# The first sequence of an attention stage in an order of its own, on one Trainium2 core

## The chip, the cores and the metric

The kernel runs on one core of a Trainium2 chip: TensorE (PE, matrix products into PSUM), VectorE (DVE), ScalarE (ACT), GpSimd (POOL), and SyncE (SP), which here only issues transfers. The metric is the device time of one execution in microseconds.

## The reference

Input x has 8 sequences of 512 tokens of 128 features. Four blocks follow, each with a layer norm before and after it and a residual. The second layer's attention is what the change is about:

```python
x = x + _layernorm(_L0_attn_ref(_layernorm(x), ...))    # a GRU with 256 hidden units over 512 steps
x = x + _layernorm(_L0_ffn_ref(_layernorm(x), ...))     # top-1 of 8 experts with low-rank parts
x = x + _layernorm(_L1_attn_ref(_layernorm(x), ...))    # below
x = x + _layernorm(_L1_ffn_ref(_layernorm(x), ...))     # SwiGLU
...
q, k, v, p, y = jnp.split(proj, ...)                    # 256 each, y: one gate for each of 16 heads
k = (1 - smear) * k + smear * k_prev
pos = jnp.cumsum(jax.nn.sigmoid(y).transpose(0, 2, 1), axis=-1)
mask = causal - (pos[..., :, None] - pos[..., None, :])
attn = softmax(q / s @ (k / s) / 4 + mask)
out = (silu(p) * (attn @ v)) @ W_out.T
```

## The kernel before

The program has three blocks, with all engines meeting between them. The first turns the GRU's weights. The second runs the recurrence, 16 steps a group, 32 groups; beside it runs the expert layer, which leaves finished rows in the tile XM, a group at a time (signal x_done), 16 steps by 8 sequences on the partitions. SyncE writes each group to the DRAM tensor x_steps and after eight groups reads a quarter of X back (L656, L661), with tokens on the partitions.

The third block is attention, sequence by sequence (b, with p = b % 2 its buffer). Its order is written out by hand in `sequences`: each engine calls the same steps, and each step has its instructions under a slot number i from 0 to 43. For a sequence there are:

- project_qk: statistics, XN (normalized rows), XT (turned), four products (two halves of q, two of k), the smearing of k on DVE (KK), and the gates, whose running sums become the columns KA and, turned, KAT.
- split (GpSimd): a float32 half becomes three bfloat16 parts, by two casts and two subtractions (PQ, PK).
- The stacks QS and KS: for each head 96 rows of parts in six orders, and rows for positions and maxima. SyncE's `project` writes parts to DRAM (q_parts, k_parts, k_extra) and reads them back turned, six loads of 256 KB for each stack. All count on one semaphore for each buffer, stack_in[p], which TensorE's `stacks` waits for as a whole before the first head.
- project_v: values and gates of the output; its bias bv3 is split in seven DVE operations (value_bias).
- maxima: for a group of four heads, 11 score products (L1730), each reduced by DVE (L2143); max_parts and rows_of_maxima bring the maxima into QS (ScalarE).
- The body of a sequence: exponentials and products with values, with the maxima two groups ahead; in its slots stand project_v of the next sequence and project_qk of the one after.

`start` does sequence 0's and 1's projections and the first two groups' maxima before the first body.

## Time and profile before

| | us |
|---|---|
| median of 3 runs | 1723.03 (1718.81 to 1726.69) |
| the profiled execution | 1728.01 |
| its span | 1726.3 |
| granted TensorE clock, mean | 0.655 |

The span is the time from first to last instruction of the one profiled execution; a clock of 1.00 is 2.4 GHz, 0.50 is 1.2 GHz. The recurrence takes the first 1053 us of the span, attention and the last block the rest.

### The profile page before, as it was taken

The page shows a single profiled execution, that of the slowest core. Times are in us where ns is not written, and L with a number is a line of the kernel's source. Part 1 is how long each engine was busy: PE and PEld are TensorE (multiplying, and loading weights), DVE is VectorE, ACT ScalarE, POOL GpSimd, SP SyncE. Part 2 cuts the span into 40 slices and gives each one's busy share as a digit, 9 for nine tenths or more (in the row PEclk, how much of TensorE's full clock was granted, in tenths as well). Part 3 has the DMA queues.
Part 4 walks back from the last instruction along what each step waited for, and adds up shares of the span by engine and source line. Part 5 has one row for each costly group of instructions (what it writes and reads, how often), then busy time and mean ns, then how long its engine had stood idle before and what let it go on. Part 6 is the DMA issues. An engine that isn't in the chain of part 4 may idle for free.

```text
span 1726.3 us, 65445 instructions
## 1 busy us (share of the span) xinstructions
PE 1403.0 (81%) x27370; PEld 1028.4 (60%) x27370; DVE 1182.0 (68%) x5759; ACT 688.4 (40%) x2427; POOL 411.8 (24%) x700
## 2 busy tenths in 40 slices
PE   5788888888888888888888774489999999988896
PEld 4677777777777777777777652245545555544443
DVE  5667777777777777777777764466577677566475
ACT  3333232222222222222222221147566666665765
POOL 2011111111111111111111124521441442411254
PEclk6555555555555555555555555679899999998898
DMA  5200000000000000000000001882563663660001
GB/s 116 25 4 5 6 5 5 6 17 7 5 5 6 5 17 6 5 7 5 5 18 5 7 6 34 103 129 33 86 87 50 94 87 48 96 87 9 1 13 37
DMA packets 68363, 55.77 MB, mean 32 GB/s; under 512 B 11086, under 2 KB 67302, under 8 KB 68070
## 3 DMA queue, kind: packets, MB, share of 16 engines
q1 hardware_dynamic: 65894, 51.41, 19.7%
q8 instruction: 215, 3.52, 0.9%
q10 hardware_dynamic: 2176, 0.20, 0.1%
q14 instruction: 78, 0.64, 0.1%
HBM read 33.93 MB, written 17.56 MB: 30 GB/s over the span
## 4 chain that ended last, share of the span: by engine, by line
PE 55%; DVE 24%; ACT 10%; issue 7%; DMA 2%; POOL 1%; SPq 0%; POOLq 0%; DVEq 0%; ACTq 0%
PE PS L716 33%; ACT tz L922 6%; DVE GB L1026 6%; DVE zg L1019 5%; PE PS L1776 5%; DVE zn L1022 4%; PE PS L1730 4%; PE PS L1746 3%; DVE MX L2143 3%; PE PS L1678 2%; ACT PT L1957 1%; PE PS L1733 1%; PE PS L1717 1%; PE PS L1749 1%; PE PS L1832 1%
## 5 line engine op out<-in xcount | busy, mean ns | idle before, releaser
L716 PE MATMUL PS<-GB,W 128*128 128x8 f16 x18432 | 575.6, 168 | 178.9 <-DVE GB L1026 174.2
L716 PEld LDWEIGHTS PS<-GB,W 128*128 128x128 f16 x18432 | 532.4, 104 | 287.6 <-DVE GB L1026 282.3
L2143 DVE TENSOR_REDUCE MX<-PS 128x1 f32<-128x512 f32 (+3 forms) x352 | 221.7, 635 | 162.8 <-PE PS L1733 160.7
L920 ACT ACTIVATE tr<-PS 128x16 f32<-128x16 f32 x512 | 93.7, 183 | 490.9 <-PE PS L716 490.9
L1957 ACT ACTIVATE PT<-PS 128x512 f32<-128x512 f32 (+1 forms) x352 | 193.1, 562 | 172.6 <-PE PS L1749 169.0
L1730 PE MATMUL PS<-KS,QS 99*128 99x256 bf16 (+3 forms) x512 | 138.6, 323 | 51.1 <-DVE MX L2143 23.7
L1012 DVE SCALAR_TENSOR_TENSOR u_<-tr,PS 128x16 f32<-128x16 f32 x512 | 87.7, 171 | 125.8 <-PE PS L716 114.2
L922 ACT ACTIVATE tz<-PS 128x16 f32<-128x16 f32 x512 | 93.7, 183 | 193.7 <-PE PS L716 193.7
L670 POOL TENSOR_TENSOR rt<-mv,eps 128x1 f32<-128x1 f32 x96 | 18.2, 190 | 553.9 <-DVE mv L1037 553.9
L1019 DVE SCALAR_TENSOR_TENSOR zg<-tz,HR 128x16 f32<-128x16 f32 x512 | 89.8, 175 | 80.6 <-ACT tz L922 80.5
L1746 PE MATMUL PS<-QS,KS 102*128 102x256 bf16 (+3 forms) x512 | 134.4, 314 | 2.8 <-ACT PT L1957 2.4
L729 PE MATMUL PS<-Y,V 128*128 128x32 f16 x2322 | 130.9, 188 | 0.0
L1730 PEld LDWEIGHTS PS<-KS,QS 99*128 99x128 bf16 x512 | 46.6, 104 | 124.7 <-DVE MX L2143 51.3
L724 PE MATMUL PS<-ones,brow 128*128 128x32 bf16 x1032 | 110.3, 188 | 2.1 <-PEq L194 2.1
L924 ACT ACTIVATE n_<-v_ 128x16 f32<-128x16 f32 x512 | 110.3, 215 | 0.4 <-DVE v_ L1016 0.2
L1776 PE MATMUL PS<-PT,VV 128*32 128x512 f32 (+3 forms) x1024 | 103.3, 477 | 1.2 <-ACT PT L1957 1.2
L1029 DVE TENSOR_TENSOR GB<-HR,GB 128x16 f16<-128x16 f32 x512 | 89.7, 175 | 17.5
L1026 DVE SCALAR_TENSOR_TENSOR GB<-zg,zn 128x16 f16<-128x16 f32 x512 | 89.5, 175 | 17.6
L1016 DVE TENSOR_TENSOR v_<-u_,PS 128x16 f32<-128x16 f32 x512 | 87.4, 171 | 17.5
L729 PEld LDWEIGHTS PS<-Y,V 128*128 128x128 f16 x2322 | 98.7, 104 | 0.0
L1733 PE MATMUL PS<-maskU,identb 128*128 128x128 bf16 x512 | 91.6, 231 | 0.0
L1022 DVE SCALAR_TENSOR_TENSOR zn<-tz,n_ 128x16 f32<-128x16 f32 x512 | 89.8, 175 | 0.6 <-ACT n_ L924 0.2
(362 smaller groups left out, 2519.2 us busy)
## 6 DMA issues: line engine op xcount, KB each, us to landing
QS<-q_parts SPq DMA_DIRECT2D x48, 256.0 KB
KS<-k_parts SPq DMA_DIRECT2D x48, 256.0 KB
q_parts<-PQ SPq DMA_DIRECT2D x16, 384.0 KB, 13.3
k_parts<-PK SPq DMA_DIRECT2D x16, 384.0 KB, 13.9
x_steps<-XM SPq DMA_DIRECT2D x32, 64.0 KB, 1.5
out_dram<-X SPq DMA_DIRECT2D x8, 256.0 KB, 2.3
X<-x_steps SPq DMA_DIRECT2D x4, 448.0 KB
XM<-in_L_attn_x_dram SPq DMA_DIRECT2D x16, 80.0 KB
```

Of the source, the lines that this page charges most:

```text
L716: return pe.matmul(bank[:, p, at:at + B], W[:, kc, w:w + P], state[:, part, kc, :], start=False, stop=True, skip_group_check=True)
L724: pe.matmul(o, brow[:, (bias + mc) * P:(bias + mc + 1) * P], ones3[:, :], start=start and mc == 0, stop=False, skip_group_check=True)
L729: pe.matmul(o, V[:, w], Y[:, rows], start=False, stop=False, skip_group_check=True)
L922: act.activation(as_states(tz), now(pZ), ACT.Tanh, scale=gate_scale).then_inc(tz_ready.sem, 1)
L1019: dve.scalar_tensor_tensor(zg[:, :], tz[:, :], 1.0, before, ALU.add, ALU.mult).then_inc(zg_ready.sem, 1)
L1022: dve.scalar_tensor_tensor(zn[:, :], tz[:, :], 1.0, n_[:, :], ALU.subtract, ALU.mult).then_inc(zn_ready.sem, 1)
L1026: dve.scalar_tensor_tensor(high, by_chunk(zg[:, :]), 0.5, by_chunk(zn[:, :]), ALU.mult, ALU.subtract).then_inc(g1_ready.sem, 1)
L1730: pe.matmul(bank[:, a * w:(a + 1) * w], QS[0:KM, p, 4 * g + i, q], KS[0:KM, p, 4 * g + i, 0:w], start=(a == 0), stop=False, skip_group_che ...
L1746: pe.matmul(bank[:, a * w:(a + 1) * w], KS[0:KF, p, 4 * g + i, j * P:(j + 1) * P], QS[0:KF, p, 4 * g + i, j * P:S], start=(a == 0), stop=F ...
L1776: last = pe.matmul(p_o[32 * i:32 * i + 32, j * P:S], VV[:, p, j, 4 * g + i, :], PT[:, j % 2, i, 0:S - j * P], start=(j == 0), stop=(j == N ...
L1957: act.activation(PT[:, j % 2, heads[0]:heads[-1] + 1, 0:w], p_e[:, k % 2, 0:len(heads) * w].rearrange("p (a w) -> p a w", w=w), ACT.Exp).t ...
L2143: dve.tensor_reduce(MX[:, g % 2, heads[0]:heads[-1] + 1, NT - 1 - it], p_x[:, k % 2, 0:len(heads) * w].rearrange("p (a w) -> p a w", w=w), ...
```

## The change

1. Finished rows go from XM to X by one transfer within SBUF for each group; the DRAM tensor is gone. SyncE's program in the second block ends when all have landed.
2. Sequence 0 has steps of its own, `first_sequence` on each engine and `project_first` on SyncE. The products go q half 0, k half 0, gates, q half 1, k half 1, into banks of their own. GpSimd splits the two q halves, DVE the two k halves.
3. The stacks of sequence 0 are read by heads: 0 to 3, 4 to 7, and 8 to 15, with a semaphore for each (the second uses x_done's, so it prints as x_rows_ready); k_extra is written and read between them.
4. value_bias runs on DVE in two pieces, around XN. The constants (tri, ones, masks) are made in the first block; KA and QA are set by DVE, VV by GpSimd between its two splits.
5. In `start`, sequence 1's project_qk comes behind the maxima of group 0 and is interleaved with those of group 1.

The core of the diff (before.py to after.py):

```diff
                 for u in range(NG):
                     sp.wait_ge(x_done.sem, u + 1)
-                    sp.dma_start(xs_d[u * GS:(u + 1) * GS].rearrange("t b d -> (t b) d"), XM[:, u, :]).then_inc(x_out.sem, 16)
-                    k = u // (NG // NT)
-                    if u % (NG // NT) == NG // NT - 1:
-                        sp.wait_ge(x_out.sem, 16 * (u + 1))
-                        for first, n, back in ((0, 1, x_back0), (1, B - 1, x_back)):
-                            sp.dma_start(X[:, k * B + first:k * B + first + n, :],
-                                         xs_d[k * P:(k + 1) * P, first:first + n, :]).then_inc(back.sem, 16)
+                    k, first = u // (NG // NT), (u % (NG // NT)) * GS
+                    sp.dma_start(X[first:first + GS, k * B:(k + 1) * B, :].rearrange("p n d -> p (n d)"),
+                                 XM[:, u, :]).then_inc(x_back.sem, 16)
+                sp.wait_ge(x_back.sem, x_back.value(sp, NG - 1))
...
                 def start():
-                    for i in range(SLOTS):
-                        project_qk(0, 0, i)
+                    first_sequence()
                     for i in range(SLOTS):
                         project_v(0, 0, i, None)
-                    for i in range(SLOTS):
-                        project_qk(1, 1, i)
                     for j in range(NT):
                         for n in range(len(ITEMS[j])):
                             maxima(0, 0, 0, j, n)
                     for k in range(NI):
                         max_parts(0, 0, 0, k)
                         rows_of_maxima(0, 0, 0, k, None)
-                    for j in range(NT):
-                        for n in range(len(ITEMS[j])):
-                            maxima(0, 0, 1, j, n)
+                    items = [(j, n) for j in range(NT) for n in range(len(ITEMS[j]))]
+                    for i in range(SLOTS):
+                        project_qk(1, 1, i)
+                        if i % 4 == 3:
+                            maxima(0, 0, 1, *items[i // 4])
...
+                def project_first():
+
+                    def out(c, parts, done, dram, src):
+                        sp.wait_ge(parts.sem, parts.value(sp, 0, 4 * (c + 1)))
+                        sp.dma_start(dram[0][:, c * P:(c + 1) * P, :].rearrange("s p n -> p s n"), src[:, c, :, :]).then_inc(done.sem, 16)
+
+                    def back(dst, dram, order, heads, done):
+                        for r, part in enumerate(order):
+                            sp.dma_start(dst[r * DH:(r + 1) * DH, 0, heads, :],
+                                         dram[0][part].rearrange("(h d) n -> d h n", d=DH)[:, heads, :]).then_inc(done.sem, 16)
+                    q_order, k_order = (0, 0, 0, 1, 1, 2), (0, 1, 2, 0, 1, 0)
+                    h0, h1, h23 = slice(0, 4), slice(4, 8), slice(8, HEADS)
+                    out(0, parts_q, q_out, qd, PQ)
+                    out(0, parts_k, k_out, kd, PK)
+                    sp.wait_ge(q_out.sem, 16)
+                    back(QS, qd, q_order, h0, first_in[0])
+                    sp.wait_ge(k_out.sem, 16)
+                    back(KS, kd, k_order, h0, first_in[0])
+                    out(1, parts_q, q_out, qd, PQ)
+                    sp.wait_ge(kaT.sem, kaT.value(sp, 0))
+                    sp.dma_start(ad[0], KAT[:, :]).then_inc(a_out.sem, 16)
+                    back(QS, qd, q_order, h1, first_in[1])
+                    sp.wait_ge(a_out.sem, a_out.value(sp, 0))
+                    sp.dma_start(KS[96:KF, 0, :, :], ad[0].rearrange("(h r) n -> r h n", r=6)).then_inc(first_in[0].sem, 16)
+                    back(KS, kd, k_order, h1, first_in[1])
+                    out(1, parts_k, k_out, kd, PK)
+                    sp.wait_ge(q_out.sem, 32)
+                    back(QS, qd, q_order, h23, stack_in[0])
+                    sp.wait_ge(k_out.sem, 32)
+                    back(KS, kd, k_order, h23, stack_in[0])
...
+                def first_sequence():
+                    scales(0)
+                    split(0, 0)
+                    pool.memset(VV[:, :, :, :, DH:32], 0.0).then_inc(acon.sem, 1)
+                    pool.wait_ge(acon.sem, 9)
+                    pool.memset(VV[:, :, :, :, DH:DH + 1], 1.0).then_inc(acon.sem, 1)
+                    split(0, 1)
+                    scales(1)
...
+                def first_sequence():
+                    pe.wait_ge(xn.sem, xn.value(pe, 0))
+                    for t in range(NT):
+                        last = pe.transpose(p_b[:, t * P:(t + 1) * P], XN[:, t, :], ident[:, :])
+                    last.then_inc(xnT_ps.sem, 1)
+                    pe.wait_ge(xnT.sem, xnT.value(pe, 0))
+
+                    def product(c, bank):
+                        pe.matmul(PS[:, bank, :], winT[:, c * P:(c + 1) * P], XT[:, 0, :], start=True, stop=True).then_inc(qk_ps.sem, 1)
+                    product(0, 7)
+                    product(2, 0)
+                    for t in range(NT):
+                        last = pe.matmul(p_a[:, t * HEADS:(t + 1) * HEADS], XT[:, 0, t * P:(t + 1) * P], winT[:, 4 * DE:], start=True, stop=True)
+                    last.then_inc(y_ps.sem, 1)
+                    product(1, 1)
+                    product(3, 2)
+                    pe.wait_ge(acon.sem, 8)
+                    pe.wait_ge(sg.sem, sg.value(pe, 0))
...
                 def stacks(b, p, g):
-                    if g == 0:
-
-                        loaded = b * (STACK_DMAS * 8) + (STACK_DMAS * 16 - STACK_DMAS * 8 * p + 16)
-                        pe.wait_ge(stack_in[p].sem, loaded if isinstance(b, int) else pe.snap(loaded))
+                    if b == 0 and g < 2:
+                        pe.wait_ge(first_in[g].sem, first_in[g].value(pe, 0))
+                    if g == (2 if b == 0 else 0):
+                        loaded = STACK_DMAS * 16 * (b // 2 + 1)
+                        pe.wait_ge(stack_in[p].sem, loaded + 16 if p else loaded - 16)
...
+                def first_sequence():
+                    act.wait_ge(xnT_ps.sem, xnT_ps.value(act, 0))
+                    act.activation(XT[:, 0, :], p_b, ACT.Identity, scale=ilw[:, 0:1], bias=ilb[:, 0:1]).then_inc(xnT.sem, 1)
+
+                    def queries(c, bank):
+                        act.wait_ge(qk_ps.sem, qk_ps.value(act, 0, 1 + turn(0, c)))
+                        act.activation(QF[:, c, :], PS[:, bank, :], ACT.Identity, scale=qsc[:, 4 + c:5 + c], bias=bqs[:, c:c + 1]).then_inc(qk.sem, 1)
+
...
+                    act.wait_ge(yb.sem, yb.value(act, 0))
+                    act.activation(SG[:, :, :], YB[:, :, :], ACT.Tanh, scale=0.5).then_inc(th.sem, 1)
+                    queries(1, 1)
+                    keys(1, 2)
...
+                dve.memset(KA[:, :, :, :], 1.0).then_inc(acon2.sem, 1)
+                dve.memset(QA[:, :, :, :], 1.0).then_inc(acon2.sem, 1)
+                value_bias((0, 1, 2))
...
+                def first_sequence():
+                    dve.wait_ge(arst.sem, arst.value(dve, 0))
...
+                    value_bias((3, 4, 5, 6))
+
+                    def smear(c):
+                        dve.wait_ge(qk.sem, qk.value(dve, 0, 1 + turn(0, 2 + c)))
...
+                    def split(c):
+                        rest = PT[:, 0, 3, :]
...
+                    smear(0)
+                    dve.wait_ge(y_ps.sem, y_ps.value(dve, 0))
+                    dve.tensor_tensor(YB[:, :, :], p_a[:, 0:NT * HEADS].rearrange("p (t h) -> p t h", t=NT),
+                                      bvpy[:, 2 * DE:].unsqueeze(1).to_broadcast([P, NT, HEADS]), ALU.add).then_inc(yb.sem, 1)
+                    split(0)
+                    dve.wait_ge(th.sem, th.value(dve, 0))
+                    dve.tensor_scalar(SG[:, :, :], SG[:, :, :], 0.5, 0.5, ALU.mult, ALU.add).then_inc(sg.sem, 1)
+                    smear(1)
```

SyncE (SP), at the first sequence's stacks, before; the shapes are partitions x heads x tokens:

```order
L1489 DMA q_parts<-PQ 128x3x512 [waits parts_ready] x2
L1492 DMA k_extra<-KAT 96x512 [waits kaT_ready]
L1497 DMA QS<-q_parts 16x16x512 [waits q_parts_to_dram]
L1497 DMA QS<-q_parts 16x16x512 x5
L1500 DMA k_parts<-PK 128x3x512 [waits parts_ready] x2
L1503 DMA KS<-k_extra 6x16x512 [waits k_extra_to_dram]
L1506 DMA KS<-k_parts 16x16x512 [waits k_parts_to_dram]
L1506 DMA KS<-k_parts 16x16x512 x5
```

and after:

```order
L1525 DMA q_parts<-PQ 128x3x512 [waits q_parts_ready]
L1525 DMA k_parts<-PK 128x3x512 [waits k_parts_ready]
L1529 DMA QS<-q_parts 16x4x512 [waits q_parts_to_dram]
L1529 DMA QS<-q_parts 16x4x512 x5
L1529 DMA KS<-k_parts 16x4x512 [waits k_parts_to_dram]
L1529 DMA KS<-k_parts 16x4x512 x5
L1525 DMA q_parts<-PQ 128x3x512 [waits q_parts_ready]
L1541 DMA k_extra<-KAT 96x512 [waits kaT_ready]
L1529 DMA QS<-q_parts 16x4x512 x6
L1544 DMA KS<-k_extra 6x16x512 [waits k_extra_to_dram]
L1529 DMA KS<-k_parts 16x4x512 x6
L1525 DMA k_parts<-PK 128x3x512 [waits k_parts_ready]
```

What was one chain of whole stacks is now three pieces, the first two of four heads each.

DVE, from the first smearing of k, before (PT is a borrowed tile that holds the value bias's parts):

```order
L2099 TENSOR_SCALAR KK<-KF_,qsc 128x512 [waits qk_ready]
L2102 SCALAR_TENSOR_TENSOR KK<-KF_,qsc,KK 128x511 [waits k_scaled]
L2099 TENSOR_SCALAR KK<-KF_,qsc 128x512 [waits qk_ready]
L2102 SCALAR_TENSOR_TENSOR KK<-KF_,qsc,KK 128x511 [waits k_scaled]
L2057 CAST PT<-bvpy 128x512
L2059 TENSOR_TENSOR PT<-bvpy,PT 128x512 [waits v_bias_parts]
L2061 CAST PT<-PT 128x512 [waits v_bias_parts]
L2063 TENSOR_TENSOR PT<-PT 128x512 [waits v_bias_parts]
L2065 TENSOR_SCALAR PT<-PT,ident 128x512 [waits v_bias_parts]
L2067 SCALAR_TENSOR_TENSOR PT<-PT,ident 128x512 [waits v_bias_parts]
L2069 SCALAR_TENSOR_TENSOR bv3<-PT,ident 128x512 [waits v_bias_parts]
```

and after, from the rest of value_bias behind XN:

```order
L2145 TENSOR_TENSOR PT<-PT 128x512 [waits v_bias_parts]
L2147 TENSOR_SCALAR PT<-PT,ident 128x512 [waits v_bias_parts]
L2149 SCALAR_TENSOR_TENSOR PT<-PT,ident 128x512 [waits v_bias_parts]
L2151 SCALAR_TENSOR_TENSOR bv3<-PT,ident 128x512 [waits v_bias_parts]
L2218 TENSOR_SCALAR KK<-KF_,qsc 128x512 [waits qk_ready]
L2220 SCALAR_TENSOR_TENSOR KK<-KF_,qsc,KK 128x511 [waits k_scaled]
L2235 TENSOR_TENSOR YB<-PS,bvpy 128x64 [waits y_ps]
L2226 CAST PK<-KK 128x512 [waits k_smeared]
L2228 TENSOR_TENSOR PT<-KK,PK 128x512 [waits k_parts_ready]
L2230 CAST PK<-PT 128x512 [waits k_parts_ready]
L2232 TENSOR_TENSOR PK<-PT,PK 128x512 [waits k_parts_ready]
L2239 TENSOR_SCALAR SG<-SG 128x64 [waits gate_tanh_ready]
```

The value bias stood between the smearing and KA; it now stands ahead, and the split of a key half has come to DVE, ahead of SG.

PE, at the end of sequence 1's projections and the first score product (PS<-KS,QS), before:

```order
L1697 MATMUL PS<-identb,KA 96x128 [waits ka_ready,qk_ready]
L1697 MATMUL PS<-identb,KA 96x128 x3
L1730 MATMUL PS<-KS,QS 128x512 [waits stacks_in0]
L1733 MATMUL PS<-maskU,identb 128x128
L1730 MATMUL PS<-KS,QS 128x512
L1733 MATMUL PS<-maskU,identb 128x128
L1730 MATMUL PS<-KS,QS 128x512 [waits max_ready]
```

and after, from the turned maxima of group 0 (identb,QA) on:

```order
L1815 MATMUL PS<-identb,QA 128x128 [waits max_parts_ready]
L1815 MATMUL PS<-identb,QA 128x128 x3
L1692 MATMUL PS<-ident,XN 128x128 [waits xn_ready,silu_ready]
L1692 MATMUL PS<-ident,XN 128x128 x3
L1786 MATMUL PS<-KS,QS 128x512 [waits max_ready,x_rows_ready]
L1789 MATMUL PS<-maskU,identb 128x128
L1700 MATMUL PS<-winT,XT 128x16 [waits xnT_ready,silu_ready]
L1700 MATMUL PS<-winT,XT 128x16 x3
L1707 MATMUL PS<-XT,winT 128x512
L1786 MATMUL PS<-KS,QS 128x512 [waits max_ready]
L1789 MATMUL PS<-maskU,identb 128x128
L1707 MATMUL PS<-XT,winT 128x512 [waits yb_ready]
```

Sequence 1's projections stood ahead of the first score product; now they stand behind the 11 of group 0, with those of group 1 between their steps.

## Rows read from the trace of the kernel before

**Rows 1.** Chain that ended last in order of time (start us, us, what), stretch 1080:1330.

```profile
1087.96 0.60 ACT KAT L1936
...
1088.98 1.04 SPq L1497
...
1093.01 14.22 DMA k_parts<-PK
...
1109.60 13.21 DMA KS<-k_parts
...
1122.85 0.61 PE PS L1730
```

**Rows 2.** Timeline, 1096 to 1172: start us, us, engine line op, idle before.

```profile
1096.15 1.11 DVE L2087 TENSOR_SCALAR XN<-X,MV,RR 128x128 f32<-128x128 f32 x4
...
1114.00 0.59 ACT L1936 ACTIVATE KAT<-PS 96x512 bf16<-96x512 bf16 x1 [6.50 <-PE PS L1697]
...
1133.47 2.42 ACT L1946 ACTIVATE QS<-PS 6x512 bf16<-6x512 bf16 x4 [18.88 <-PE PS L1759]
...
1141.75 0.63 PE L1746 MATMUL PS<-QS,KS 102*128 102x512 bf16 x1
...
1171.21 0.38 PE L1730 MATMUL PS<-KS,QS 99*128 99x512 bf16 x1
```

**Rows 3.** Timeline, 1052 to 1068, all engines and SyncE's queue.

```profile
1052.93 0.32 SPq L656 DMA_DIRECT2D x_steps<-XM  x1
...
1054.47 0.80 SPq L661 DMA_DIRECT2D X<-x_steps  x2
...
1056.31 0.87 DVE L2049 BATCH_NORM_STATS2 STa<-X 128x6 f32<-128x128 f32 x4 [0.44 <-DMA X<-x_steps]
...
1059.15 2.48 DVE L2087 TENSOR_SCALAR XN<-X,MV,RR 128x128 f32<-128x128 f32 x4 [1.54 <-POOL RR L139]
...
1059.17 1.80 POOL L1534 MEMSET VV<- 128x2048 f32 x1
...
1063.73 1.89 PE L1671 MATMUL PS<-winT,XT 128*128 128x16 f32 x8 [0.93 <-ACT XT L1919]
...
1065.45 6.64 PE L1678 MATMUL PS<-XT,winT 128*128 128x512 f32 x8
...
1067.54 0.78 ACT L1925 ACTIVATE QF<-PS,bqs,qsc 128x512 f32<-128x512 f32 x1 [3.87 <-PE PS L1678]
```

**Rows 4.** One line's instructions in all: duration ns min/median/max.

```profile
L1568 POOL TENSOR_TENSOR RES<-QF,PQ x16: 1152/1157/1476, 1069.2 to 1477.4; 128x512 f32<-128x512 f32 x16
...
L1570 POOL CAST PQ<-RES x16: 609/610/720, 1070.5 to 1478.7; 128x512 bf16<-128x512 f32 x16
...
L2099 DVE TENSOR_SCALAR KK<-KF_,qsc x16: 473/475/1394, 1071.7 to 1482.1; 128x512 f32<-128x512 f32 x16
```

**Rows 5.** Stretches: length, busy us of each engine, granted clock, DMA share, GB/s.

```profile
core 0: us, PE busy (x) PEld busy (x) DVE busy (x) ACT busy (x) POOL busy (x), PEclk, DMA share, GB/s
...
1097.00:1101.00 4.00, 2.64 (x13) 2.46 (x14) 0.37 (x2) 0.78 (x1) 0.00 (x0) 0.72 1.15 115
...
1130.00:1142.00 12.00, 9.49 (x47) 4.50 (x48) 8.75 (x17) 2.35 (x4) 0.00 (x0) 0.50 1.04 154
...
1144.00:1148.00 4.00, 3.75 (x28) 2.39 (x28) 3.43 (x10) 3.10 (x7) 0.00 (x0) 1.00 1.16 116
```

**Rows 6.** Tile q_parts: time of its writes from issue to landing.

```profile
DMA to landing us min/median/max: 2.5/13.3/14.2
```

**Rows 7.** Timeline: SyncE's stack loads of sequences 1 and 2, TensorE's wait.

```profile
1124.51 2.80 SPq L1497 DMA_DIRECT2D QS<-q_parts  x6
...
1141.73 2.80 SPq L1506 DMA_DIRECT2D KS<-k_parts  x6
...
1197.09 2.85 SPq L1497 DMA_DIRECT2D QS<-q_parts  x6
...
1232.03 0.59 PE L1730 MATMUL PS<-KS,QS 99*128 99x512 bf16 x1 [1.95 <-issue]
```

180 lines of the change are left out of this document (109 added, 71 removed).

## The prediction

> **What bounds the kernel now.** I read the page first: a profiled execution of 1728.0 us, span 1726.3 (the table above). The recurrence of the first layer takes the first 1053 us, and nothing of the change costs time in it. So I read the chain of work that ended last only behind it, in order of time. There the chain leaves the engines: ScalarE copies KAT, the position rows of the keys, at 1087.96, SyncE issues the query loads at 1089.0, then come 14.2 us of the transfer k_parts and 13.2 us of the transfer into KS, and TensorE's first score product starts at 1122.85 [rows 1]. From 1089.0 to 1122.85, 33.9 us, TensorE does the value projection and sequence 1's projections, and then it stands still. The reader is to see that one thing ends that stretch: all 16 heads of both stacks must have landed before the first head is scored. The steady part (from 1141.75, exp products of sequence 0 on TensorE [rows 2]) is TensorE's own, and the change leaves it as it is; so what counts is when it starts, and whether sequence 1's stacks are there when it asks for them.
>
> **The row transfers.** Before, the last rows went to DRAM at 1052.93, had landed when the loads back were issued at 1054.47 (1.54 us), and DVE's statistics started at 1056.31 [rows 3]. After, one transfer of 64 KB within SBUF, and SyncE ends its program when it has landed. No row shows such a transfer; I take the 1.54 us of its neighbour. The other engines then start some 0.8 us earlier (the two issues of rows 3 are gone), and the statistics at about 1055.2: 1.1 us gained. Bounds: 0 (it lands 1.1 us later) and 1.4. The deletions inside the recurrence are hidden beside 2 us steps that do not wait for SyncE: nothing. The constants of GpSimd go to the first block, behind its last work there: at most a fraction of a microsecond of DVE contention, taken as nothing.
>
> **Up to the first parts.** XN starts at 1059.15 and its four pieces take 2.48, since GpSimd's clearing of VV (1.80) starts beside them [rows 3]; sequence 1's four take 1.11 [rows 2]. After, DVE does two memsets and three value-bias steps in the wait (some 2.5 us by estimate, 0.5 each, against 1.54 of waiting), so XN starts near 1059.4 and ends at 1060.5 instead of 1061.6. Transposes and XT take what they took (2.1 us), the first product no longer stands behind the gate products (they start at 1063.73, the first product at 1065.45 [rows 3]: 1.7 us), so QF is there 2.8 us earlier, at 1064.75 instead of 1067.54. GpSimd splits the first query half in two casts of 0.61 and two subtractions of 1.15 to 1.48 with gaps [rows 4]: done at 1069.9. The first key half follows in 1.7 us on TensorE (four products in 6.64 [rows 3]): KF_ at 1067.2, smeared by DVE at 1069.4. Its split on DVE is four operations of the kind of L2099, 0.475 alone and 1.39 beside GpSimd [rows 4]; VV's 1.8 us memset now lies beside them. I take 1.2 each with gaps: done at 1074.4; bounds 1071.5 and 1076.5. KA follows at 1079.1, the second key half at 1081.9, moments at 1083.2. So KAT comes 8 us earlier, at 1080.
>
> **The first stack.** A write of one half (384 KB) lands in 2.5 us when nothing is ahead of it, and the loads run at 115 GB/s [rows 5, 6]. Four heads of QS are 384 KB: 3.4 us at that rate, and as six issues 2.8 us of SyncE (six took 2.80 [rows 7]). In the order of the queue: q half written 1070.0, k half 1074.5, QS heads 0 to 3 issued 1075.0 to 1078.0, KS of them to 1080.9, second query half, k_extra at 1081.5, QS heads 4 to 7 to 1084.5; the wait for k_extra in DRAM ends near 1085.5, and KS's rows of it, behind 384 KB in the queue, land near 1090.5. TensorE comes to the scores at about the same time: KA is there at 1079, but DVE takes the value projection up only at 1083.3, and its four chunks end at 1090. First score product 1090.5 instead of 1122.85. The heads 4 to 15 (2.3 MB) are all in by 1104, ahead of their use.
>
> **What takes the time back.** Sequence 1's projections ran inside the old wait; now they stand behind the maxima of the first four heads. From the first score product to the last row of maxima on ScalarE are 13.0 us (1122.85 to 1133.47 + 2.42 [rows 1, 2]): 1103.5. There ScalarE takes XT of sequence 1; from there to KAT were 15.9 us (1098.1 to 1114.0, XN's end plus 0.8 [rows 2]), now with six maxima between the steps. Eleven took at most 13.0 - 2.4 = 10.6 us, 0.96 each; I count half of that, since the rest falls into waits (bounds: nothing and all, 0 and 5.8): KAT at 1122.3. Five more maxima, 3.7 us: the steady part starts at 1126.0 instead of 1141.75, 15.7 us earlier. Next is late: sequence 1's stacks. They are asked for 29.5 us behind the start (1141.75 to 1171.21 [rows 2]), so at 1155.5. From the issue of the query loads to their landing were 33.9 us for sequence 0 [rows 1] and 34.9 for sequence 2 (1197.09 to 1232.03, where TensorE waited 1.95 [rows 7]); sequence 1's KS was issued 17.2 us behind its first issue (1124.51, 1141.73 [rows 7]), which with 14.3 us to land makes 31.5. With the first issue at 1122.6, behind KAT: 1154.1 to 1157.5, a wait of 0 to 2. I take 1. The 15 us of slack that sequence 1 had are spent.
>
> **The sum.** 15.7 - 1 = 14.7, some 15 us: 1713.3 for a profiled execution like the one of 1728.0, which stood 5.0 above the median; so 1708 for the median of 1723.0.
>
> **The rivals.**
> 1. The forecast, 11 to 19 us gained (1704 to 1712): 0.54.
> 2. More, 19 to 26 us (about 1700). TensorE's granted clock was 0.50 (1.2 GHz) while it alternated with DVE in the maxima and 1.00 (2.4 GHz) in the steady part [rows 5]. With the projections and maxima of heads 4 to 7 interleaved it is fed more densely; at the high level their 22 us shrink by 3 or 4, and the six maxima may hide wholly (3). Against: sequence 1's stacks move by this only as far as KAT does. 0.13.
> 3. The small loads cost more. Each of the 24 loads of four heads is 64 KB. If such a load took 0.95 us of the queue instead of the 0.56 that 115 GB/s gives, the 12 ahead of the first score product would end 4.7 us later: 10 us gained, 1713. With the issues also stretched, or the wait for k_extra longer, 5 to 11 gained (about 1714). 0.17. For: the queue is a chain of four round trips here. Against: twelve issues hide the load.
> 4. Sequence 1's stacks come 4 to 9 us late, since the writes of its key halves stand behind 1.5 MB of query loads (14.2 us to land [rows 1]): 5 to 10 gained, 1715. 0.10. It is decided by KAT of sequence 1: every microsecond past 1122 in it counts once.
> 5. Slower. The interleaved projections stretch, because each hop between engines now waits behind a maximum on DVE and TensorE, and KAT of sequence 1 comes so late that its stacks land behind 1171.2, when they were asked for before. That decides from KAT at 1137 on; at 1147 the kernel ends 10 us later, 1733. Against: six maxima at 0.96 us are 5.8 us, so it would take over three times their length. 0.03.
> 6. Nothing: the wait for the first stack is only renamed (first_stacks_in lands past 1110): 1720. 0.03.
>
> Beside rival 3: the Trainium skill, "DMA: Bandwidth & Descriptors", section "Measured (HBM→SBUF, 128 partitions, SWDGE, issued from GpSimd)", gives 0.95 us for 64 KB and advises transfers of 1 MiB or more, which speaks against cutting the loads. By it the sum would be 10 instead of 15. These are SyncE's queues, and the trace has 256 KB loads at 115 GB/s, far under that page's rate for such sizes, so I leave it the smaller chance.
>
> **How the numbers follow.** Runs of this kernel spread by 0.5%, 8.6 us, which is also about what a measurement can tell from no change. Cases 1 and 2 are faster by more (0.67), and of cases 3 and 4 (0.27) somewhat under half: 0.78 faster, 0.19 the same, 0.03 slower. The range goes from 1699, which takes in most of rival 2, to 1718, which takes in rivals 3 and 4 and the spread of the runs; it leaves out cases 5 and 6 and the tail of 2, about 0.12.
>
> **What would show it.** Right: the first score product near 1090, released by KS (k_extra) or by the value projection within 3 us of each other; KAT of sequence 1 at 1120 to 1124; the first exp product at 1124 to 1128; the first maxima of sequence 1 behind a wait of 0 to 2 us; from there a constant shift. Wrong: a first score product past 1097 (rival 3), a wait over 4 us for sequence 1's stacks (rival 4), KAT past 1130 (rival 5), or DVE's split of the first key half past 1077, which would put every transfer off.

## The result, and the profile after

Measured together, the changed kernel took 1708.67 us (median of 6 runs, 1701.6 to 1716.0) and the kernel before 1724.86 (6 runs, 1717.39 to 1727.86): a ratio of 0.9923, 95% interval 0.9894 to 0.9952. That is 13.3 us won (8 to 18) by the ratio, 16.2 by the medians. The forecast was 1708.

The page of the changed kernel's profiled execution (1701.6 us) shows that its engines do the same work; the queue q1 has fewer bytes, since the row transfers no longer go through DRAM, and the clock row reads 9 in the recurrence, where the execution before read 5 (the last line is that of before):

```profile
PE 1397.2 (82%) x27355; PEld 1028.8 (61%) x27370; DVE 1180.2 (69%) x5769; ACT 688.0 (40%) x2427; POOL 404.3 (24%) x690
...
PEclk9999999999999999999999999789999999999898
...
q1 hardware_dynamic: 65126, 49.31, 18.7%
```

```profile
PEclk6555555555555555555555555679899999998898
```

The timeline at the entry of the attention block, changed kernel (start us, us, engine line op):

```profile
1051.23 0.45 POOL L712 TENSOR_TENSOR XM<-XM,N 128x128 f32<-128x128 f32 x1 [0.18 <-POOL N L709]
...
1051.70 0.55 SPq L675 DMA_DIRECT2D X<-XM  x1
...
1054.60 0.87 DVE L2127 BATCH_NORM_STATS2 STa<-X 128x6 f32<-128x128 f32 x4
...
1058.21 1.11 DVE L2211 TENSOR_SCALAR XN<-X,MV,RR 128x128 f32<-128x128 f32 x4
```

The recurrence ends with the addition to XM, at 1051.68 here and at 1052.90 before. To compare executions, every mark below is counted from there. Statistics start 2.92 us behind it instead of 3.41 [rows 3], and XN's four pieces take 1.11 us instead of 2.48.

The timeline of the same execution at the marks that the prediction named; a bracket holds the idle time ahead and what ended it:

```profile
1086.98 0.39 PE L1786 MATMUL PS<-KS,QS 99*128 99x512 bf16 x1 [2.83 <-DMA KS<-k_extra]
...
1097.33 2.42 ACT L2024 ACTIVATE QS<-PS 6x512 bf16<-6x512 bf16 x4 [12.30 <-PE PS L1815]
...
1116.35 0.59 ACT L1994 ACTIVATE KAT<-PS 96x512 bf16<-96x512 bf16 x1 [6.38 <-PE PS L1724]
...
1121.09 0.63 PE L1802 MATMUL PS<-QS,KS 102*128 102x512 bf16 x1
...
1153.79 0.38 PE L1786 MATMUL PS<-KS,QS 99*128 99x512 bf16 x1
```

The first score product came at 1122.85 [rows 1] and comes at 1086.98, where the extra key rows are the last thing it waits for (2.8 us). The first exp product came at 1141.75 and the first maxima of sequence 1 at 1171.21 [rows 2]; now 1121.09 and 1153.79. So 35.9 us are won at the first score product, 20.7 at the first exp product and 17.4 at sequence 1's maxima (1.2 of each is the recurrence's). The stretch between the last two marks, called the body below, covers the first two of sequence 0's four groups of four heads. It grew from 29.5 to 32.7 us: 2.7 us of that is TensorE standing idle (1.3 us before, 4.0 now), 0.5 us is its busy time. The chain in order of time says what it stood idle for, which had not been foreseen:

```profile
1082.84 4.09 DMA KS<-k_extra
...
1120.92 0.62 POOL PK L1590
1121.61 1.17 POOL PK L1592
1123.24 1.03 POOL RR L146
1124.30 0.60 DVE XN L2171 x2
1124.90 0.61 DVE MX L2272
1125.64 0.58 PE PS L1786
```

```profile
1125.64 0.58 PE L1786 MATMUL PS<-KS,QS 99*128 99x512 bf16 x1 [2.67 <-DVE MX L2272]
```

The last step of GpSimd's splits of sequence 1, before:

```profile
1119.85 1.15 POOL L1572 TENSOR_TENSOR PK<-RES,PK 128x512 bf16<-128x512 f32 x1
```

Before, these splits ended 20.7 us ahead of the first exp product; now they run from 1105.6 to 1122.8 and end 1.7 us behind it. Behind them on GpSimd stand the scales of sequence 2; DVE waits for these with XN, and behind XN in DVE's order stands the maximum that TensorE waits 2.67 us for.

### The profile page after: what moved, and what is told of

Same layout as the page of the kernel before. It is cut to its first block and busy times, and to the rows that moved or that the text cites. A ratio compares the mean times of both kernels' runs of the same rounds, so it can differ in the third digit from the quotient of the medians.

```text
span 1699.8 us, 65434 instructions
## 1 busy us (share of the span) xinstructions
PE 1397.2 (82%) x27355; PEld 1028.8 (61%) x27370; DVE 1180.2 (69%) x5769; ACT 688.0 (40%) x2427; POOL 404.3 (24%) x690
```

## The experiments

Each kernel is the changed one with one edit, unless said otherwise. The marks, in us from the end of the recurrence, one profiled execution each; "body" is the last mark less the one ahead of it, with TensorE's mean granted clock in it and the longest single wait for DVE in it. Ratios are to the kernel before, with 95% intervals; runs with the same letter were made together, each letter on a chip of its own, so ratios rather than medians compare across letters.

| kernel | first score | first exp | seq. 1's maxima | body | clock | wait | median us | ratio |
|---|---|---|---|---|---|---|---|---|
| before | 69.95 | 88.85 | 118.31 | 29.5 | 0.98 | 0.97 | 1719.3 to 1724.9 | 1 |
| changed | 35.30 | 69.41 | 102.11 | 32.7 | 0.94 | 2.67 | 1708.67 | 0.9923 (0.9894 to 0.9952) |
| e1 whole stacks | 49.77 | 83.47 | 119.83 | 36.4 | 0.82 | 2.29 | 1722.35 | 1.001 (0.999 to 1.003) |
| e2 old order of the start | 52.63 | 71.56 | 100.85 | 29.3 | 0.99 | 0.96 | 1703.06 | 0.9909 (0.9878 to 0.9941) |
| e3 one splitter | 36.03 | 70.42 | 105.59 | 35.2 | 0.80 | 1.68 | 1707.42 | 0.9932 (0.9908 to 0.9957) |
| e4 eight heads | 41.27 | 74.80 | 107.85 | 33.1 | 0.91 | 2.38 | 1712.36 | 0.9951 (0.9928 to 0.9974) |
| f1 scales early | 35.50 | 68.90 | 99.40 | 30.5 | 0.99 | 1.29 | 1703.08 | 0.988 (0.9842 to 0.9917) |
| f2 extra key rows early | 33.28 | 66.93 | 102.01 | 35.1 | 0.80 | 1.68 | 1708.59 | 0.992 (0.9892 to 0.9948) |
| f3 rows through DRAM | 36.08 | 69.19 | 105.46 | 36.3 | 0.82 | 2.27 | 1707.08 | 0.9903 (0.9865 to 0.9942) |
| f4 both interleaved, f1 and f2 | 34.60 | 65.32 | 96.72 | 31.4 | 0.89 | 0.97 | 1698.61 | 0.9865 (0.9833 to 0.9896) |
| g1 changed, once more | 35.50 | 69.85 | 107.91 | 38.1 | 0.73 | 1.68 | 1709.26 | 0.9928 (0.9899 to 0.9957) |
| g2 f2 with extra products | 33.35 | 68.28 | 101.58 | 33.3 | 0.90 | 1.92 | 1710.07 | 0.9912 (0.9878 to 0.9946) |
| g3 both interleaved | 35.58 | 65.56 | 95.29 | 29.7 | 0.95 | 0.97 | 1699.61 | 0.986 (0.982 to 0.99) |
| g4 value bias whole | 38.62 | 72.88 | 107.96 | 35.1 | 0.81 | 1.68 | 1712.28 | 0.9955 (0.993 to 0.998) |

Two executions of the very same kernel (changed, g1) agree within 0.5 us at the first two marks and differ by 5.8 at the third. So the first two marks read single edits; the third and the total need the body's clock beside them.

**e1, the first score product waits for the whole stacks.** (The stacks have sixteen heads; in the expectation they were miscounted as twelve, and in e4's the pieces are eight and eight against four, four and eight.)

```
-                    if b == 0 and g < 2:
-                        pe.wait_ge(first_in[g].sem, first_in[g].value(pe, 0))
-                    if g == (2 if b == 0 else 0):
+                    if b == 0 and g == 0:
+                        pe.wait_ge(first_in[0].sem, first_in[0].value(pe, 0))
+                        pe.wait_ge(first_in[1].sem, first_in[1].value(pe, 0))
+                    if g == 0:
```

> The changed kernel, but TensorE takes its first score product of the first sequence only when the stacks of all twelve heads are in, instead of four heads' at a time. Theory (the wait for the first stack is what the change took away, and everything behind it follows): the last pieces of the stacks are issued at 1089.6 to 1092.3 us and would land at 1095 to 1098, so the first score product goes from 1086.98 to about 1096, the first exponential's product from 1121.1 to about 1130, and the kernel is 8 to 10 us slower than the changed one, near 1717. Rival (the time was won by the new order of the start, and the stacks would have been in time for it): the first exponential's product moves by under 3 us, the time by nothing that can be told.

The first score product of e1 on TensorE, and the step ahead of it in the chain:

```profile
1101.22 0.58 PE L1786 MATMUL PS<-KS,QS 99*128 99x512 bf16 x1 [16.03 <-DMA KS<-k_parts]
```

```profile
1091.72 9.37 DMA KS<-k_parts
```

It came 14.3 to 14.5 us later, not 9: the last piece, issued at 1091.7, took 9.4 us to land. The kernel is as fast as the one before, with every other part of the change in it. The theory holds, and its 8 to 10 us were too small (15 us by the ratios). The other parts are not idle, though: the first exp product is 5.4 us ahead of the kernel before's (83.47 against 88.85), and the body, 36.4 us instead of 29.5, takes all of it back.

**e2, the old order of the start.**

```
+                    for i in range(SLOTS):
+                        project_qk(1, 1, i)
                     for j in range(NT):
                         for n in range(len(ITEMS[j])):
                             maxima(0, 0, 0, j, n)
...
-                    for i in range(SLOTS):
-                        project_qk(1, 1, i)
-                        if i % 4 == 3:
-                            maxima(0, 0, 1, *items[i // 4])
+                    for j in range(NT):
+                        for n in range(len(ITEMS[j])):
+                            maxima(0, 0, 1, j, n)
```

> The changed kernel with the old order at the start: the whole projection of the second sequence ahead of the first maxima, and the six maxima of group 1 behind those of group 0 in one piece, not one after every fourth step of the projection. Theory: the interleaved order hides the six maxima in the projection's waits (some 5 us won) but starts the projection 10 us later, at the end of the first maxima, and its halves are then split too late, so that GpSimd's scales of the third sequence come late in the first body; the old order starts the projection at about 1085 while the stacks are under way. The two nearly cancel: first exponential's product 1120 to 1124 against 1121.1, first body back at 29.5 to 30.5 us against 32.7, its maxima of the second sequence at 1150 to 1154 against 1153.8. Rival (the interleaving carries a large part of the gain): 5 us or more later at both places.

The body of e2, one row of the windows (stretch, us, busy time of PE, PEld, DVE, ACT, POOL, then clock, DMA share, GB/s):

```profile
1124.60:1153.89 29.29, 27.76 (x241) 15.84 (x239) 20.47 (x49) 19.41 (x36) 14.77 (x16) 0.99 0.56 82
```

The rival fell. The first exp product is 2 us later, and the body is back at 29.3 us, at a clock of 0.99 and with no wait for GpSimd's scales, which were done at 1114.4; at sequence 1's maxima the old order is 1.3 us ahead of the best execution of the new one. The two orders are worth about the same: in the old one the projection fills the wait for the stacks, in the new one it hides about half of group 1's eleven maxima.

**e3, GpSimd splits all four halves.** DVE's `split(0)` and `split(1)` become GpSimd's `split(0, 2)` behind its first and `split(0, 3)` behind its second.

> The changed kernel with all four halves of the first sequence's queries and keys split by GpSimd, none by DVE. Theory: GpSimd's split of the first key half ends at about 1072.8 instead of 1071.7, but its query half 2 slips from 1078.8 to about 1083, and with it, on SP's queue, the extra rows of the keys that the first score product waits for: 1088.5 to 1091 against 1086.98, and the first exponential's product 2 to 4 us later. Rival (the sharing between two engines carries the gain): 8 us later or more. Second rival (DVE's own chain behind its splits matters more): no later, or earlier, since the extra rows are computed about 4 us sooner.

On SyncE's queue of e3 the key half is written at 1073.72 against 1071.71 in the changed kernel, and the extra rows' read goes out at 1084.05 against 1082.84. The recurrence ended 0.64 us later in this execution, so the differences are 1.4 and 0.6 us:

```profile
1073.72 0.40 SPq L1525 DMA_DIRECT2D k_parts<-PK  x1
...
1084.05 0.33 SPq L1544 DMA_DIRECT2D KS<-k_extra  x1
```

0.5 to 0.7 us later at the first score product, 0.6 to 1.0 at the first exp product, and no difference in the time. The theory (2 to 4 us) and the first rival (8) both expected more; the second rival (no later) is nearer. Without DVE's splits GpSimd ran its casts and subtractions mostly at their short lengths (0.61 and 1.15), so the queue as a whole came only half a microsecond later. Halves split by two engines are worth under 1 us.

**e4, pieces of eight heads.** `h01, h23 = slice(0, 8), slice(8, HEADS)`, and the two loads of heads 4 to 7 are gone.

> The changed kernel reading the first stacks in pieces of eight and four heads instead of four, four and four: 12 fewer transfers (6 of queries, 6 of keys), each of the first ones twice as large. Theory (small transfers are nearly free on this path, the wait is for the extra rows of the keys): SP reaches the extra rows' read up to 1 us earlier and the first score product stands between 1085.5 and 1089. Rival (each small transfer costs about its issue time and occupies the queue): the 12 saved ones are worth 2 us or more at the first score product and at the first exponential's. Second rival (reading by four heads is what gets the first score product so early): eight heads' pieces land late, first score product at 1090 or later.

SyncE's queue of e4, and the first score product:

```profile
1078.91 0.48 SPq L1541 DMA_DIRECT2D k_extra<-KAT  x1
1088.79 0.30 SPq L1543 DMA_DIRECT2D KS<-k_extra  x1
```

```profile
1092.71 0.61 PE L1784 MATMUL PS<-KS,QS 99*128 99x512 bf16 x1 [8.79 <-DMA KS<-k_extra]
```

12 fewer transfers, and 5.8 to 6.0 us later. SyncE had issued the write of k_extra at the same time as in the changed kernel (1078.91 against 1079.31), but it took 9.9 us to land instead of 2.9. From the transfer tables of the changed kernel and of e4 (KB, us from issue to landing):

```profile
k_extra<-KAT SPq DMA_DIRECT2D x1, 96.0 KB, 2.9
```

```profile
k_extra<-KAT SPq DMA_DIRECT2D x1, 96.0 KB, 9.9
```

Twelve loads stand ahead of it in both, 1.5 MB in e4 and 768 KB in the changed kernel. SyncE issues twelve in 6.5 to 6.7 us either way. At four heads the DMA engines keep up with that (their busy share from 1077 to 1081 is 0.65); at eight heads they do not (1.17, at 125 GB/s), and the small write waits for the backlog. So the bytes ahead count, not the transfers. The Trainium skill ("DMA: Bandwidth & Descriptors", section "Queues, rings and completion order") has each DMA engine take a ring's descriptors in their order; the rows agree. Its advice in the section on measured bandwidth is transfers of 1 MiB or more; the step in that direction, from 64 to 128 KB, cost 6 us here, where a small transfer behind the loads ends the wait.

**f1, moments and scales of sequence 2 ahead of the first value projection.**

```
                     moments_out(1)
+                    dve.wait_ge(aaggr.sem, aaggr.value(dve, 1))
+                    for t in range(NT):
+                        moments(2, t)
+                    moments_out(2)
...
                     scales(1)
+                    scales(2)
```

The slots of sequence 1's projection that did them before leave them out.

> The changed kernel with the moments and scales of the third sequence (2.4 us of DVE, 1.3 us of GpSimd) done ahead of the first sequence's value projection and not behind GpSimd's splits of the second one. Theory (the first body lost some 3 us because GpSimd's late splits held the scales back, and TensorE waited 2.67 us at 1125.64 behind DVE): that wait goes, the stretch from the first exponential's product to the second sequence's first maxima is 29.5 to 31 us instead of 32.7; the first score product is not over 1 us later than 1086.98, since it waits for the extra key rows anyway; the second sequence's first maxima come 1 to 3 us earlier than 1153.8. Rival (the first body was longer for another reason, such as GpSimd's splits or DMA traffic themselves): the stretch stays at 32 us or more, and the start is up to 2.4 us later.

The body of f1, the same kind of row, and sequence 1's first maximum behind it:

```profile
1120.16:1150.66 30.50, 27.92 (x240) 15.90 (x239) 21.51 (x49) 19.75 (x36) 16.50 (x18) 0.99 1.07 142
```

```profile
1150.66 0.38 PE L1787 MATMUL PS<-KS,QS 99*128 99x512 bf16 x1 [0.15 <-issue]
```

As the theory had it: 30.5 us at a clock of 0.99, the third mark 2.7 us ahead of the better execution of the changed kernel, and the median, 1703.1, below those of f2 and f3 made with it. A wait of 1.29 us is left there. And f1 stands at the next limit: the last of sequence 1's stack loads landed at 1150.57, 0.1 us ahead of the product that needs it.

**f2, the extra key rows ahead of the query rows of heads 4 to 7.** In `project_first`, the write of ad and its read stand ahead of `back(QS, qd, q_order, h1, first_in[1])`, with the second query half between them.

> The changed kernel with SP's queue in another order for the first sequence: the extra key rows are written and read ahead of the query rows of heads 4 to 7, not around them. Theory (with reading by eight heads the first product came 6 us later, waiting for these rows behind twice the bytes, so bytes queued ahead of them count): they are read 1 to 2 us sooner and with 384 KB less ahead of them, and the first score product stands at 1085 to 1086, where the value projection ends; everything behind it 1 to 2 us earlier. Rival (the rows' own latency counts, not what is ahead of them): under 0.5 us.

SyncE and TensorE in f2:

```profile
1078.26 0.42 SPq L1540 DMA_DIRECT2D k_extra<-KAT  x1
...
1080.23 0.30 SPq L1543 DMA_DIRECT2D KS<-k_extra  x1
```

```profile
1084.42 0.39 PE L1786 MATMUL PS<-KS,QS 99*128 99x512 bf16 x1 [0.84 <-DMA KS<-k_extra]
```

Won: 2.0 to 2.2 us at the first score product and 2.5 to 2.9 at the first exp product, more than the 1 to 2 expected. The body then took 35.1 us, and the time is that of the changed kernel.

**f3, the rows through DRAM again.** The two trips of before stand in SyncE's last loop, with their waits on DVE.

> The changed kernel with the last layer's rows moved through DRAM again, as before, and not within SBUF. Theory (after the change the block's entry stood 2.8 us behind the last row transfer, as before it, and the statistics began 0.5 us sooner at most): the first transposes of the first sequence stand 0 to 0.6 us later behind the end of the recurrence than 7.7 us, and the time is the same. Rival (the prediction's step): 1.1 us later. Second rival (two trips through DRAM cost what the page shows for them, over 2 us each): 2 us or more.

```profile
1053.59 0.32 SPq L678 DMA_DIRECT2D x_steps<-XM  x1
1055.13 0.80 SPq L682 DMA_DIRECT2D X<-x_steps  x2
```

```profile
1056.96 0.87 DVE L2133 BATCH_NORM_STATS2 STa<-X 128x6 f32<-128x128 f32 x4 [0.43 <-DMA X<-x_steps]
```

The recurrence ended at 1053.56 in it: statistics at 3.40 us (2.92 in the changed kernel), the first transposes at 8.18 (7.66 to 7.70). As the theory had it; both rivals fell. The transfer within SBUF is worth 0.5 us at the entry, and nothing of it is to be seen in the time.

**f4 and g3, sequence 1's projection interleaved with the maxima of both groups.** g3 is this edit alone; f4 has f1's and f2's as well.

```
-                    for j in range(NT):
-                        for n in range(len(ITEMS[j])):
-                            maxima(0, 0, 0, j, n)
-                    for k in range(NI):
-                        max_parts(0, 0, 0, k)
-                        rows_of_maxima(0, 0, 0, k, None)
-                    items = [(j, n) for j in range(NT) for n in range(len(ITEMS[j]))]
+                    items = [(g, j, n) for g in range(2) for j in range(NT) for n in range(len(ITEMS[j]))]
                     for i in range(SLOTS):
                         project_qk(1, 1, i)
-                        if i % 4 == 3:
-                            maxima(0, 0, 1, *items[i // 4])
+                        if i % 2:
+                            maxima(0, 0, *items[i // 2])
+                        if 0 <= i - 2 * NI < NI:
+                            max_parts(0, 0, 0, i - 2 * NI)
+                            rows_of_maxima(0, 0, 0, i - 2 * NI, None)
```

> The changed kernel with more put together: the second sequence's projection begins at once behind the first value projection and is interleaved with the maxima of both first groups, one after every second step (group 0's eleven, then group 1's, with the rows of maxima of group 0 beside the latter), together with the early scales of the third sequence and the early extra key rows. Theory (the projection's chain is mostly latency in which DVE and TensorE have room for the eleven maxima of group 0, 9.6 us, and the rows of maxima, 2.5 us, hide as well): first exponential's product at 1111 to 1116 instead of 1121.1, first body at 29.5 to 31 us, second sequence's first maxima 1141 to 1147 instead of 1153.8, and the kernel 7 to 12 us faster than the changed one. Rival (the maxima and the projection hold each other up on DVE, where both are in one order): first exponential's product at 1119 or later, and under 3 us won.

> The changed kernel with the second sequence's projection interleaved with both groups' maxima, without the early scales and the early extra key rows. Theory (of the 4.1 us that the first exponential's product came earlier with all three, the extra key rows carry 1 to 2 us and the interleaving 2 to 3; the early scales only shorten the first body): first exponential's product 66 to 68 us behind the recurrence's end, against 69.4, and the second sequence's first maxima 97 to 100 us behind it. Rival (the interleaving itself is worth nothing, being bound by DVE): 69 us or more.

The body of g3:

```profile
1117.18:1146.91 29.73, 28.47 (x240) 16.39 (x239) 20.59 (x49) 19.46 (x36) 14.78 (x16) 0.95 0.81 125
```

f4 won 4.1 us at the first exp product, g3 alone 3.9: the rival fell, and the interleaving is worth more than the 2 to 3 us expected of it. f1 and f2 add nothing that can be told at this mark. In f4 the first score product no longer waits for the key rows but follows the value projection, ahead of which f1's DVE work stands; that f2's 2 us are lost to this is argued from the rows, not tried. The projection now starts 9.5 us earlier (its first transposes at 36.6 instead of 46.1), so GpSimd's splits are done in time (at 1112.1, 5.1 us ahead of the first exp product), and the body is back at 29.7 us. f4's body took 31.4, since its clock fell to 0.50 for some 3 us near its end. g3's 1699.6 us (1697.6 to 1703.4) stands against 1709.3 (1704.9 to 1718.3) of the changed kernel on the same chip (4 runs and 9): all of its runs are faster than all of the changed kernel's. It is 1.4% below the kernel before, as f4 is.

**g1, the changed kernel once more.**

> The changed kernel itself once more, as the mark on this chip for the others of this call and to see how its landmarks repeat: the first score product 35 to 36 us behind the recurrence's end, the first exponential's product 69 to 70 us, ratio 0.990 to 0.995. The first body (32.7 us) by the theory of the clock varies with the stretch of 1.2 GHz that falls into it, 30 to 36 us, and the wait behind GpSimd's scales stays at 1.5 to 3 us; by the rival it repeats within 0.5 us.

The bodies of the changed kernel in both executions (g1 second), and that of before:

```profile
1121.09:1153.79 32.70, 28.70 (x240) 16.67 (x239) 21.31 (x49) 19.42 (x36) 17.59 (x20) 0.94 1.02 138
```

```profile
1122.20:1160.26 38.06, 35.41 (x241) 19.51 (x240) 21.46 (x49) 19.57 (x36) 17.52 (x20) 0.73 0.87 118
```

```profile
1141.75:1171.21 29.46, 28.15 (x241) 15.96 (x240) 20.63 (x49) 19.42 (x36) 14.78 (x16) 0.98 0.60 82
```

The same instructions; DVE and ACT are as busy in both executions, TensorE's busy time is 35.4 us in g1 in place of 28.7, at a mean clock (the third column from the right) of 0.73 in place of 0.94. So the body was outside the 30 to 36 us expected, and the rival (it repeats within 0.5 us) fell too. Of what g1's body is longer than that of before, 7.3 us are TensorE's busy time and 1.3 its waits; in the first execution it was 0.5 and 2.7. In both the clock fell to 0.50 some 6 to 7 us ahead of the body, in a wait for the columns KA of sequence 1. The line of that wait in the changed kernel, then the same in g1 and g1's wait in the body:

```profile
1115.68 0.63 PE L1724 MATMUL PS<-identb,KA 128*96 128x128 bf16 x4 [3.46 <-DVE KA L2205]
```

```profile
1116.79 0.63 PE L1724 MATMUL PS<-identb,KA 128*96 128x128 bf16 x4 [3.88 <-DVE KA L2205]
1126.75 0.58 PE L1786 MATMUL PS<-KS,QS 99*128 99x512 bf16 x1 [1.68 <-DVE MX L2272]
```

In the first execution it rose within 1 us of the body's start and fell again in the wait of 2.67 us. In g1 it had not risen when its wait of 1.68 us came, and stood at 0.50 for 17 us of the body. So g1's loss did not begin with the wait in its body, and how much of the body runs at 1.2 GHz differs between executions of one kernel.

**g2, f2's kernel with products that nothing reads in TensorE's waits.** It computes more than is asked for.

```
                     max_item(b, p, g, it, n)
+                    if b == 0 and g == 1:
+                        for _ in range(12):
+                            pe.matmul(p_o[:, 0:P], identb[:, :], maskU[:, :], start=True, stop=True)
```

> The kernel with the early extra key rows, and in addition TensorE computes twelve products of 128 columns that nothing reads behind each of the eleven maxima's score products that stand beside the second sequence's projection, where it otherwise waits for DVE. Theory (the first body took 35.1 us there and 32.7 in the changed kernel, not 29.5, chiefly because TensorE had waited much beforehand and its granted clock was 0.50 for the first 13 us of it): with the waits filled the granted clock of the first body is 0.9 or more and the body takes 30 to 32 us, while the products delay the first exponential's product by 0 to 3 us behind 66.9 us. Rival (the body's length comes from waits behind DVE and GpSimd, the clock only follows them): the body stays at 34 us or more, and the added products are a loss.

Windows of 5 us from 1116 on, g1 first, then g2, whose body begins 3.6 us later (its recurrence ended at 1057.48):

```profile
1116.00:1121.00 5.00, 3.72 (x20) 2.11 (x21) 4.49 (x15) 0.59 (x1) 4.23 (x6) 0.50 0.46 144
1121.00:1126.00 5.00, 4.07 (x20) 2.02 (x18) 3.04 (x7) 1.79 (x3) 3.84 (x5) 0.50 1.16 115
1126.00:1131.00 5.00, 4.25 (x19) 2.70 (x20) 3.73 (x11) 1.88 (x4) 0.00 (x0) 0.50 1.14 112
1131.00:1136.00 5.00, 5.00 (x20) 3.02 (x22) 1.19 (x3) 0.95 (x3) 0.00 (x0) 0.50 1.08 216
```

```profile
1116.00:1121.00 5.00, 3.63 (x55) 3.17 (x55) 4.79 (x16) 0.59 (x1) 4.31 (x5) 1.00 0.22 79
1121.00:1126.00 5.00, 5.00 (x82) 4.64 (x80) 3.28 (x9) 0.00 (x0) 4.23 (x6) 1.00 0.94 134
1126.00:1131.00 5.00, 3.04 (x22) 1.56 (x20) 3.68 (x11) 2.34 (x4) 1.77 (x3) 0.99 1.14 118
1131.00:1136.00 5.00, 5.00 (x20) 3.31 (x19) 1.83 (x5) 2.03 (x4) 0.00 (x0) 0.50 1.13 166
```

Half right. With the extra products (x55 and x82 instead of about x20) the clock stood at 0.99 to 1.00 until 1131. The body began at 1125.8, TensorE waited 1.92 us for DVE up to 1129.4, and behind that the clock fell to 0.50 all the same, for about 7 us. Its mean over the body was 0.90, as forecast, but the body took 33.3 us (35.1 without), outside the forecast 30 to 32; the first exp product came 1.4 us later, and the time did not move. The wait itself has to go. The Trainium skill ("TensorE: Matmul & The Clock Gate", Part 1) has the clock fall behind idle stretches of the engine and rise with activity, at a phase that differs from run to run; the two executions of one kernel agree with it in that they differ. The recurrence (last section) shows where the clock costs nothing.

**g4, the value bias in one piece.** `value_bias(range(7))` where the first three steps stood, nothing behind XN.

> The changed kernel with all seven steps of the value bias in one piece ahead of the normalisation of the first sequence, where the first three stand in the change. Theory (the first three hide in DVE's wait for the scales, the last four in its wait for the first key half; in one piece their 4 instructions of about 0.5 us stand on the path): the first transposes come 1.5 to 2.5 us later than 7.7 us behind the recurrence's end, and everything behind them as much. Rival (another wait of as much takes it up before the first score product): under 0.7 us at the first score product.

The start of XN in g4, whose recurrence ended at 1051.81:

```profile
1061.24 1.11 DVE L2211 TENSOR_SCALAR XN<-X,MV,RR 128x128 f32<-128x128 f32 x4
```

9.4 us behind the recurrence instead of 6.5: 2.9 us late (1.5 to 2.5 expected), 3.1 to 3.3 at the first score product and 3.0 to 3.5 at the first exp product. Nothing takes it up. In the time it is 3.0 us by the medians beside g1, which the intervals do not part. The placing of four DVE instructions is worth more than the split by two engines and the row transfers together.

## Why the prediction was right

Total, direction and range were right. The way to the first exp product came out 3.7 us better than forecast, and the body behind it 2.2 us worse in one execution and 7.6 in the other. That the two cancelled, so that 1708 was met to a microsecond, is luck. The profiled execution shows it: it was forecast at 1713.3 and took 1701.6. For comparison with the times of the prediction, 1.22 us is added to those of the changed profile, since its recurrence ended so much earlier.

- **Row transfers: mis-sized.** 1.1 us forecast, 0.5 measured (2.92 against 3.41 us, and f3). The step that failed is that the other engines start 0.8 us earlier: the next block's first instructions start 2.8 us behind the issue of the last transfer out of XM in both kernels (1051.70 to 1054.48, 1052.93 to 1055.67). What went is DVE's wait of 0.44 us for the rows.
- **Up to the first parts: right to 0.1 us** for XN's end (1060.5 forecast, 1060.5), QF (1064.75, 1064.75) and the first query half (1069.9, 1069.9). The key half was forecast for 1074.4 and was there at 1072.9. Within its bounds; the four operations of its split took 0.69 to 1.26 us instead of 1.2 each. KA 1079.1 against 1078.0.
- **First stack: right in its cause, 2.3 us off.** 1090.5 forecast, 1088.2 measured, released by KS (k_extra), with the value projection done 1.5 us ahead, as the test asked. SyncE read the extra rows at 1084.1, not 1085.5, and they landed 4.1 us behind that, not 5. e4 shows why this term was worth its care: the order and the bytes in SyncE's queue decide it.
- **What takes the time back: over-sized.** First score product to the rows of maxima: 13.0 forecast, 12.8 measured. The interleaved maxima were counted at 2.9 us and cost 0.7 (XT's start to KAT 16.6 instead of 15.9 us): nearly all fell into waits. So KAT of sequence 1 stood at 1117.6, not 1122.3. The five maxima behind it were put at 3.7 us, for which the prediction gives no working (at its own 0.96 each they make 4.8), and took 4.7. So the first exp product stood at 1122.3, not 1126.0. At this mark 19.4 us were won and 15.7 forecast.
- **Next is late: right about the stacks, but something else came first.** A wait of 1 us for sequence 1's stacks was put in. None is seen in the trace, but only just: KS's loads go out from 1136.00 to 1138.8, the last lands at 1152.10 (1153.3 in the prediction's times, which had 1154.1 to 1157.5), and the maxima ask at 1153.79. Had the body kept its 29.5 us they would have asked at 1150.6 and waited 1.5 us. The stacks are the limit next in line, as f1 shows. What the prediction left out is GpSimd: its splits of sequence 1, which the prediction moved along with everything else without asking what stood behind them on GpSimd, hold up sequence 2's scales. The body is 3.2 us longer for it in the profiled execution, most of it the wait, and 8.6 in g1, most of it the clock. e2, f1, f4 and g3, where the scales are not behind late splits, have 29.3 to 31.4.
- **The sum.** 14.7 us forecast at sequence 1's maxima; 16.2 in one profile and 10.4 in the other, 13.3 on average, and 13.3 by the ratio. Behind that mark the fourteen executions of the table took 547 to 557 us to their end, without order among the kernels: a constant shift as forecast, with a spread of 9 us that is the runs' own. The kernel before has the longest of them (556.8) and the changed one nearly the shortest (547.7), which is why the two profiles differ by 26 us.

Of the rivals, 3 (small loads cost more) is refuted by the first score product, which came ahead of the forecast and not 4.7 us behind it, and by e4, where fewer and larger loads were 6 us slower. 4 (sequence 1's stacks late) did not happen. 2 was right about the hidden maxima, but not about the clock: it did not rise. From 1090 to 1121 it was 0.50 but for some 7 us, much as before. 6 is what e1 gives: without the reading by heads the rest of the change, in its own order of the start, is worth nothing in time. Whole stacks with the old order of the start were not tried.

By parts, then, at the first exp product: reading by four heads 14 us; the value bias in two pieces and not all ahead of XN 3.0 to 3.5 (its old place, behind the smearing, was not tried); two splitters 0.6 to 1.0; rows within SBUF 0.5 at the entry, nothing certain later; the interleaved order 1.7 to 2.2, given back in the body. The parts were taken away one at a time, so they need not add up. The new order of the products and the moved clearing of VV (XN is 1.37 us shorter without it) were not taken away by themselves; by the rows, QF starts 2.8 us sooner.

The clock's part is shown as a relation, not as a cause. In the nine executions whose scales stood behind late splits, 4 to 20 us of the body ran at 0.50; in the five others (before, e2, f1, f4, g3) it was at 1.00 within 4 us of the start and stayed, but for f4's late fall. In five of the nine (changed, e1, e4, f3, g2) it had risen, or not fallen, and fell in or just behind the wait of 1.9 to 2.7 us. In the other four (e3, f2, g1, g4) it had not risen since the wait for KA ahead of the body. f1 took away wait and clock loss together; and the wait of 0.97 us late in every body was followed by a fall in two executions of fourteen (f4, g1).

## What to carry to other kernels

When a long wait goes, list for every engine what used to run inside it, and for each of these what stands behind it in its engine's order: the work does not vanish, it comes out late somewhere else (here GpSimd's splits, then the scales behind them). In a queue where a small transfer ends a wait, count the bytes ahead of it rather than the transfers: 768 KB more ahead of 96 KB cost 6 us, and another order in the queue won 2. A chain of short steps on several engines has room for independent work in its gaps (some five reductions for 0.7 us in the changed kernel, nine for 0.9 in g3), so interleave all of it and start the chain early. Read single edits at marks counted from a common point; the total hides anything under 5 us.
